# A fused eight-layer kernel: two PSUM banks for the scan's turned states, its end states kept by ScalarE, the causal mask added by VectorE, and another order for the feed-forward parts beside the scan

## The reference, cut to what matters

```python
x = x + _L0_attn_a_ref(_layernorm(x), ...)   # attention, 32 heads of 16
x = x + _L0_ffn_ref(_layernorm(x), ...)      # feed-forward, 1376 inner columns
x = x + _L0_attn_b_ref(_layernorm(x), ...)   # state-space layer with a scan
x = x + _L0_ffn_ref(_layernorm(x), ...)      # the same feed-forward again
x = x + _L1_attn_a_ref(_layernorm(x), ...)   # grouped attention, 32 heads of 128, rotary, causal
x = x + _L1_ffn_ref(...)                     # routed low-rank layer
x = x + _L1_attn_b_ref(...)                  # gated layer that zeroes the smaller half
x = x + _L1_ffn_ref(...)

# the scan of _L0_attn_b_ref: 1024 channels x 16 states, 512 tokens in order
def step(state, inp):
    dt_t, B_t, C_t, u_t = inp
    dA = jnp.exp(dt_t[..., None] * A)
    state = state * dA + (dt_t * u_t)[..., None] * B_t[:, None, :]
    y = jnp.einsum('bdn,bn->bd', state, C_t)
    return (state, y)

# the feed-forward, and the mask of _L1_attn_a_ref
gate = silu(x @ w_gate.T + b_gate); up = x @ w_up.T + b_up
out = (gate * up) @ w_down.T + b_down
scores = scores + jnp.where(qpos[:, None] >= kpos[None, :], 0.0, finfo(float32).min)
```

## Time and profile before

| | |
|---|---|
| median of 3 runs | 3086.19 us (3082.8 to 3101.64) |
| the profiled execution | 3082.76 us, its span 3081.0 us |
| granted TensorE clock over the span | 0.885 of full speed |
| busy over the span | PE 2444.4, DVE 2010.7, ACT 1585.7, POOL 1151.9 us |

### The profile page before, as it was taken

One profiled execution on the slowest core, in us unless ns is written; L12 is line 12 of the kernel. 1 busy time (PEld: TensorE's weight loads), 2 busy tenths in 40 slices (PEclk: granted clock), 3 DMA queues, 4 the chain that ended last, 5 costly groups with the idle time before them and its releaser, 6 DMA issues.

```text
span 3081.0 us, 36657 instructions
## 1 busy us (share of the span) xinstructions
PE 2444.4 (79%) x12408; PEld 1919.7 (62%) x12408; DVE 2010.7 (65%) x3083; ACT 1585.7 (51%) x3190; POOL 1151.9 (37%) x1016
## 2 busy tenths in 40 slices
PE   6986989677678857867889799999799999952058
PEld 4334358566667646756678678887678877842046
DVE  4724743587677569767754567775667774498894
ACT  1641640366665236666621166664366664599701
POOL 3011046051122424112247547565555754510071
PEclk8887899788898979888999999999899999976579
DMA  6123223110100111010023202111111112200011
GB/s 216 43 90 90 43 69 93 42 45 4 61 22 25 48 53 34 11 59 21 22 61 93 76 25 59 45 52 52 48 35 49 59 45 59 69 28 0 0 31 45
DMA packets 87696, 155.72 MB, mean 51 GB/s; under 512 B 8824, under 2 KB 17656, under 8 KB 87384
## 3 DMA queue, kind: packets, MB, share of 16 engines
q1 hardware_dynamic: 87512, 153.38, 17.2%
HBM read 138.21 MB, written 14.75 MB: 50 GB/s over the span
## 4 chain that ended last, share of the span: by engine, by line
PE 36%; ACT 9%; DVE 5%; issue 4%; POOL 2%; POOLq 0%; ACTq 0%; DVEq 0%
PE ps L623 33%; ACT tables L1290 5%; PE ps L637 3%; ACT m L1173 1%; POOL w_lo L567 1%; ACT tables L1145 1%; POOL w_hi L566 1%; POOL k L580 1%; DVE stat L1344 0%; DVE tables L1767 0%; DVE hT_lo L1357 0%; DVE f_lo L1329 0%; DVE x_sb L1332 0%; DVE f_hi L1328 0%; ACT m L1155 0%
## 5 line engine op out<-in xcount | busy, mean ns | idle before, releaser
L566 POOL TENSOR_SCALAR w_hi<-w_in 128x512 fp32r<-128x512 f32 x430 | 324.6, 755 | 1387.8 <-PE ps L623 822.3
L567 POOL TENSOR_TENSOR w_lo<-w_in,w_hi 128x512 fp32r<-128x512 f32 x430 | 614.1, 1428 | 35.9
L623 PE MATMUL ps<-hT_hi,w_lo 128*128 128x512 f32 x864 | 352.9, 408 | 22.9 <-DVE a L1374 12.5
L1533 DVE TENSOR_TENSOR_SCAN m<-m,m 128x1028 f32<-128x1028 f32 x128 | 307.8, 2404 | 69.7 <-ACT m L1173 62.3
L637 PE MATMUL ps<-tables,m 128*128 128x128 f32 x1024 | 186.1, 311 | 205.4 <-ACT tables L1145 121.0
L623 PE MATMUL ps<-hT_hi,w_hi 128*128 128x512 f32 x864 | 341.9, 396 | 0.0
L623 PE MATMUL ps<-hT_lo,w_hi 128*128 128x512 f32 x864 | 341.4, 395 | 0.0
L623 PE MATMUL ps<-m,tables 128*128 128x128 f32 (+1 forms) x2112 | 323.5, 302 | 12.7 <-ACT tables L1145 12.0
L623 PEld LDWEIGHTS ps<-m,tables 128*128 128x128 f32 (+1 forms) x2112 | 293.5, 213 | 22.6 <-ACT tables L1145 16.3
L637 PEld LDWEIGHTS ps<-tables,m 128*128 128x128 f32 x1024 | 128.5, 157 | 241.3 <-ACT tables L1145 144.5
L1145 ACT ACTIVATE tables<-ps 128x512 f32<-128x512 f32 x256 | 150.7, 589 | 189.0 <-PE ps L637 185.5
(11 more groups left out here) (245 smaller groups left out, 5470.4 us busy)
## 6 DMA issues: line engine op xcount, KB each, us to landing
w_in<-units SPq DMA_DIRECT2D x430, 256.0 KB, 2.6
stack_scratch<-a SPq DMA_DIRECT2D x48, 256.0 KB
a<-stack_scratch SPq DMA_DIRECT2D x64, 192.0 KB, 4.5
m<-bc_scratch SPq DMA_DIRECT2D x16, 512.0 KB, 5.3
out<-x_sb SPq DMA_DIRECT2D x2, 1024.0 KB, 4.3
tables<-small SPq DMA_DIRECT2D x1, 1399.0 KB, 10.5
x_sb<-x SPq DMA_DIRECT2D x4, 256.0 KB, 3.6
x_sb<-x SPq DMA_DIRECT2D x1, 1024.0 KB, 7.6
```

Source lines behind the costliest of these rows:

```text
L566: c["did"](nc.gpsimd.tensor_scalar(w_hi[:, r], raw, 1.0, 1.0, ALU.mult, ALU.mult), s["unit_hi"])
L567: c["did"](nc.gpsimd.tensor_tensor(w_lo[:, r], raw, w_hi[:, r].bitcast(F32), ALU.subtract), s["unit_split"])
L623: ins = T.matmul(out, lhsT, rhs, start=start, stop=stop)
L1533: V.tensor_tensor_scan(states, m_dA[:, dA:dA + NG].rearrange("p a t -> p (a t)"), states, 0.0, ALU.mult, ALU.add)\
```

## The change

Scan:

- the turned states of part 0 stay in bank 6, those of part 1 go to bank 5; the up projection beside the scan moves from bank 5 to bank 4, where it follows the gate;
- `m_dA` has 3 groups of buffers, and ACT makes the decays of group n+1 in group n's turn, ahead of both copies of turned states of n-2;
- the end states of the first half are kept by ACT (`last_kept`) and put back by ACT (in `decays`); both DVE copies are gone;
- the time steps of the second half's first tiles are made during the last tile of the first half, as between any tiles;
- on DVE `skip` comes behind the next group's inputs.

Feed-forward: the gate is an item of its own (`fgate`), and the order on PE is gate k, down k-1, up k everywhere. ACT's silu stands at the up item. Beside the scan `at_ends` puts the parts [gate k, down k-1], [up k], [multiply k] in the middle and at the end of the 16 tiles; of the second batch's scan, block 0 now stands ahead of the scan.

Grouped attention: the mask matmuls are gone, and DVE adds the mask to the last 128 columns of t = 1, 2, 3 in PSUM (`hide`) before the maxima.

To make room, `m_ssmT` and `m_v` lie over the routing weights, and one table (`Bw`) is loaded again ahead of the grouped attention, whose first users wait for it.

```diff
+            s += [[("fgate", b, k, up)], [("fproj", b, k, up)], [("fmul", b, k, up)]] if k < FK else []
+            s[-3 if k < FK else -1] += [("fdown", b, k - 1)] if k else []
...
+    def at_ends(scans, parts):
+        out, done, ends = [], 0, 2 * DT
+        for n, item in enumerate(scans):
+            out.append(item)
+            tile, last = divmod(n, N_ST // QS)
+            want = (2 * tile + last + 1) * len(parts) // (2 * ends) if last else done + ((tile + 1) * len(parts) // ends - tile * len(parts) // ends) // 2
+            out += flat(parts[done:want])
+            done = want
+        return out + flat(parts[done:])
...
-    s += front(1) + ln(0) + mix(scan(1), ffn(0))
+    s += front(1) + ln(0) + flat(ffn(0)[:3]) + at_ends(scan(1), ffn(0, 4)[3:])
...
-                if q == 0 and i % 2 and i + 1 < DT:
+                if q == 0 and i % 2 and (half, i) != (1, DT - 1):
                     time_steps(i + 1)
...
-                    o, slot = claim(6, s["m_hT_kept"]), n % G_RING * NG + 2 * part
+                    o, slot = claim(6 - part, s["m_hT_kept"]), n % G_RING * NG + 2 * part
...
+                def last_kept(n):
+                        act.wait_ge(s["m_h"], n + 1)
+                        go(A(m_last[:, st:st + NG].unsqueeze(2), m_st[:, slot:slot + NG, HL:SEG], ACT.Copy), s["m_last_kept"])
...
+                def decays(n):
+                    if n >= DA_RING:
+                        act.wait_ge(s["m_h"], n - DA_RING + 1)
+                    if at >= DT * N_ST // NG:
+                        act.wait_ge(s["m_last_kept"], lasts_kept(n - DT * N_ST // NG))
+                        go(A(m_st[:, slot:slot + NG, 0:1], m_last[:, st:st + NG].unsqueeze(2), ACT.Copy), s["m_dA"])
+                    for r in range(NG):
+                        go(A(m_dA[:, n % DA_RING * NG + r, 1:SEG], m_dt[:, tile % 4], ACT.Exp, scale=negA[:, st:st + 1]), s["m_dA"])
...
                 for g in range(q * QS // NG, (q + 1) * QS // NG):
                     n = scan_group(b, half, i, g)
-                    if n - 2 >= first:
-                        states_kept(n - 2, 0)
+                    decays(n + 1)
+                    last_kept(n - 2)
                     if i == 0:
                         diagonal(g)
                     if n - 2 >= first:
+                        states_kept(n - 2, 0)
                         states_kept(n - 2, 1)
...
-                    if held:
-                        skip()
                     after = following(g)
                     if after[1:] != (0, 0):
                         inputs(*after)
-                    if half == 0:
-                        did(V.tensor_copy(m_last[:, at:at + NG].unsqueeze(2), m_st[:, slot:slot + NG, HL:SEG]))
+                    if held:
+                        skip()
...
-                            mm(o[:, t * P:w], ident_r[:, :], mask_r[:, :], False, True, s["g_scores"])
...
                 def maxima_2():
                     need(s["g_scores"])
+                    go(hide(2))
+                    need(s["g_scores"])
+                    did(hide(3))
                     go(top(2))
-                    need(s["g_scores"])
                     did(top(3))
```

More of the change, by code:

```diff
@@ L59 @@
 SEG = HL + 1
-G_RING = 3
+G_RING, DA_RING = 3, 3
 G_KEEP = G_REP + 2
@@ L82, in schedule, with ffn, flat @@
     s = []
-    def ffn(b):
+    def ffn(b, up=5):
         s = []
         for k in range(FK + 1):
-            s += [("fproj", b, k), ("fmul", b, k)] if k < FK else []
-            s += [("fdown", b, k - 1)] if k else []
-        return s
+            s += [[("fgate", b, k, up)], [("fproj", b, k, up)], [("fmul", b, k, up)]] if k < FK else []
+            s[-3 if k < FK else -1] += [("fdown", b, k - 1)] if k else []
+        return s
+    def flat(parts):
+        return [item for part in parts for item in part]
     def scan(b):
@@ L156, in item_units @@
         return [("ao", c) for c in range(HC)]
+    if kind == "fgate":
+        return [("fg", item[2])]
     if kind == "fproj":
-        return [("fg", item[2]), ("fu", item[2])]
+        return [("fu", item[2])]
     if kind == "fdown":
@@ L194, in scan_group, with decays_made, lasts_kept @@
     return ((2 * b + half) * DT + i) * (N_ST // NG) + g
+def decays_made(n):
+    per = DT * N_ST // NG
+    return NG * (n + 1) + n // (2 * per) * per + max(n % (2 * per) + 1 - per, 0)
+def lasts_kept(n):
+    per = DT * N_ST // NG
+    return n // (2 * per) * per + min(n % (2 * per) + 1, per)
 def columns(widths):
@@ L328, in hybrid_layers @@
         m_acc = cut("m_front", 1024, 2)
-        m_ssmT = cut("m", 512)
+        m_ssmT, m_v = (small[:, SMALL["route_A"][0] + 512 * n:SMALL["route_A"][0] + 512 * (n + 1)] for n in range(2))
+        m_v = m_v.rearrange("p (a c) -> p a c", a=2)
         m_ssm, m_sq = cut("m_front", TT * 64, TT), cut("m_front", TT * 64, TT)
@@ L1144, in states_kept @@
                         act.wait_ge(s["m_y"], 2 * n + part - 1)
-                    go(A(m_hT[:, part], ps[:, 6], ACT.Copy), s["m_hT_kept"])
+                    go(A(m_hT[:, part], ps[:, 6 - part], ACT.Copy), s["m_hT_kept"])
                 def diagonal(g):
@@ L1597, in top, with hide @@
                     return V.reduce_max(g_max[:, t:t + 1], ps[:, bank, at_s:at_s + (t + 1) * P] if src is None else src, AX.X)
+                def hide(t):
+                    bank, at_s = g_bank[t]
+                    own_keys = ps[:, bank, at_s + t * P:at_s + (t + 1) * P]
+                    return V.tensor_tensor(own_keys, own_keys, col("mask"), ALU.add)
                 def shifts(t):
```

106 lines of the change are left out of this document (55 added, 51 removed).

## The result

The changed kernel takes 3064.61 us (median of 8 runs, 3053.74 to 3075.57), the kernel before beside it 3086.69 us (8 runs, 3076.89 to 3115.04). The ratio is 0.9918, with a 95% interval of 0.9893 to 0.9944. The forecast was 2980, a fall of 106 us; a fifth of it came, and the time lies above the range. The profiled execution took 3064.25 us, its span 3062.5, against 3081.0 before.

What follows compares the result with a forecast made beforehand. Scans were bound by no engine (DVE nearest), other stages by PE. 3081 - 107 (scans) + 3 (second scan's start) + 9.5 (feed-forward) - 11.5 (mask) = 2975 span, 2980 as median; range 2925 to 3045.

Steps and rivals of the forecast that it cites:

- What bounds the kernel: Whole kernel: in the scans no engine is full, DVE nearest; feed-forward alone and grouped attention are set by PE.
- Scan, DVE's work: Each scan: both copies leave DVE, saving 15 us (8 to 22.8), so its work falls from 307.5 to 292.5 us.
- Scan, DVE's idle time: Each scan: DVE's idle time falls from 96.5 to 58 us, the sum of 8, 12, 16 and 22.
- Skip: Scans: DVE's skip, moved behind the next inputs, waits 8 us for PE's outputs instead of 31 (bounds 0 and 16).
- Decays: Scans: decays made a group ahead cut the scan's wait for ACT from 31 to 12 us (5 to 20).
- Silu, time steps, start of the second half: Scans: DVE's remaining waits at these places fall from 34 to 16 us (10 to 26).
- New wait at the inputs: Scans: DVE's inputs wait for turned states behind PE's double feed-forward blocks, 22 us (0 to 70).
- Scan, ACT and banks: Scans: ACT's 64 added small copies, at most 19 us, fit its idle time; 3.2 us per group against DVE's 3.5.
- ACT's order: Scans, rival: copies behind four decays close a ring, 5.2 us per group, 428 per scan, 3135 in all; chance 0.04.
- Start of the second scan: Ahead of the second scan: gate 0, up 0 and the multiply lengthen the chain by 3 us (0 to 8).
- Feed-forward alone: Outside the scans: PE stalls 0.5 us for f_lo's split in each of 9 + 10 blocks, +9.5 us (0 to 19).
- Mask: Grouped attention: 192 matmuls less on PE, -11.5 us; DVE's 192 additions, 54 us, fit its idle time.

Runs made afterwards that it cites:

- e9: Kernel before, with the feed-forward taken out of the scans and put behind each: 3091.55 us (one run); first scan 315.3 us.
- e10: Changed kernel, but DVE again keeps and puts back the end states, as before: 3058.01 us, ratio 0.9886.
- e6: Changed kernel, but ACT makes both copies of turned states and its copy of the end states ahead of decays and diagonals: 3022.32 us, ratio 0.9778.
- e12: Changed kernel with e1, e2, e6 and e7 together, and one feed-forward part behind each scan item: 2971.58 us, ratio 0.9612.
- e7: Changed kernel, but the time steps' product is made at the end of the tile before, ahead of the feed-forward part: 3044.9 us, ratio 0.9851.
- e4: Changed kernel, but down k-1 stands with the multiply everywhere, so PE's blocks beside the scans are single ones of 12 matmuls: 3081.5 us, ratio 0.9972.
- e1: Changed kernel, but SP asks for three more weight units ahead of the transfers that broadcast B and C: 3065.75 us, ratio 0.9919.
- e11: Changed kernel, but second batch's block 0 is inside the scan again, and the first scan's last multiply stands earlier: 3083.97 us (one run).
- e2: Changed kernel, but the feed-forward that stands alone has its old order on PE (gate k, up k, down k-1): 3049.7 us, ratio 0.9868.
- e5: Changed kernel, but both parts of the turned states go to bank 6, as before the change: 3153.79 us, ratio 1.0203.

## Why the prediction was wrong

**What bounds the kernel.** Right: the scans are nobody's, heads and feed-forward are PE's. Missed: how poor the scans' overlap is. The earlier trace rows had the sign of it: 404 us with 302 of PE, and ten blocks beside it of some 8 us of PE each; I never asked what the scan would take without them. e9 says 315, so the last 82 us of that scan are bought at full price.

**Scan, DVE's work.** Forecast 292.5, measured 294.5. Right. But that the time would fall with it was assumed; in e10 DVE has 6.6 us more of it and the scans are no longer (2 us less, within what they vary), with ACT's order as in the change.

**Scan, DVE's idle time: the step that failed.** Forecast 58, measured 83.5. The forecast took it that decays ahead of both copies cost nothing, since ACT's 3.2 us of a group fit into DVE's 3.5; with the copies first (e6) a scan is 17.5 us shorter, out of 28 that each scan misses. By its terms, in the second scan (they add up to 81.8 of its 87.8 us of idle time):

- *Skip*, forecast 8, measured 23.9. I took 1.2 us off each of 13 waits and let PE "come sooner once it need not wait for its bank". It did not: PE now waits for ACT's copies at the outputs. But late copies are not the whole cause. With the copies first the skip still waits 27.6 (e6) and 29.3 (e12), so the 8 was wrong for a reason that no run here isolates.
- *Decays*, forecast 12, measured 2.1. Right and better than forecast. It was got by putting them first on ACT, which the inputs paid for; e6 has them second at 7.3.
- *Silu, time steps, start of the second half*, forecast 16, measured 10.8 + 14.6 = 25.4. The boundary itself did go as said: 11.0 us from scan to scan instead of 23.7.

```profile
1339.95 2.30 DVE L1582 TENSOR_TENSOR_SCAN m<-m,m 128x1028 f32<-128x1028 f32 x1
...
1350.97 3.26 DVE L1582 TENSOR_TENSOR_SCAN m<-m,m 128x1028 f32<-128x1028 f32 x1
```

  What was not seen is that the product for each next pair of tiles stands behind a block of 24 feed-forward matmuls at some places (e7: 9 us a scan). That is no fault of the change alone: ACT waited 28.1 us for it before and 40.6 after. The forecast let this wait shrink, and it grew.
- *New wait at the inputs*, forecast 22, measured 21.7 + 8.7 = 30.4. The first part is what was forecast in size, but not by its cause: with blocks of half the length it is 23.8 (e4), and e6, which leaves the blocks alone, takes it down to 6.5. The 8.7 is the wait for ACT's copy of the end states, which stands behind the decays; in e6 it is 1.3. I had priced that copy by its length and not by its place in the queue.

**Scan, ACT and banks.** The size was right (19 at most). The small copies take 0.2 us, 12.7 us in a scan:

```profile
L1213 ACT ACTIVATE m<-m 128x4 f32<-128x4 f32 x32 | 6.5, 205 | 10.7 <-DVE m L1536 5.9 <-DVE m L1582 4.5
L1175 ACT ACTIVATE m<-m 128x4 f32<-128x4 f32 x32 | 6.2, 195 | 0.0
```

The rule was wrong. The rival *ACT's order* I gave 0.04, since ACT's share of a group (3.2 us) stays below DVE's 3.5. That is a mean over an undisturbed group. At a time step or a silu ACT has some 10 us in one piece (1187.52 to 1197.62 above), and there the copies wait behind all of it; e6 shows 17.5 us a scan for the order. So it was a milder form of the rival, not the closed ring of 5.2 us in each group. That the 17.5 us lie at the places with a time step or a silu (7 and 10 in a scan) is my reading of the one place shown; no run separates them.

**Start of the second scan.** Forecast +3, measured +15.2. PE comes to gate 0 with nothing split:

```profile
1131.70 0.62 POOL L594 TENSOR_SCALAR w_hi<-w_in 128x512 fp32r<-128x512 f32 x1 [58.88 <-DMA w_in<-units]
```

```profile
1122.99 11.03 SPq L482 DMA_DIRECT2D w_in<-units  x5
```

```profile
1133.76 0.76 PE L651 MATMUL ps<-hT_hi,w_lo 128*128 128x512 f32 x1 [6.97 <-issue]
```

SP asks for these weights at 1122.99, behind the broadcasts of B and C, and they land 8.7 us later; the gate starts 7 us late, its first eight matmuls 0.43 us apart (0.23 later). e1 gives 5 of the 12 us back; the rest is the work itself, which e11 pays inside the scan (12.5) when it is not here. I counted the block as work of PE alone and not its weights' way through SP and POOL.

**Behind the scans, not priced:** +8.5 and +5.4. The last multiply and down stand behind the last scan item and must go through skip, DVE and PE one after the other. Here is that place in the first batch; in e12, where they stand ahead of the last scan item, these stretches are 69.8 and 81.7:

```profile
1005.64 0.69 DVE L1382 TENSOR_TENSOR f_lo<-loose,f_hi 128x512 fp32r<-128x512 f32 x1
```

```profile
1006.39 0.50 PE L651 MATMUL ps<-w_hi,f_lo 128*128 128x512 f32 x1 [2.55 <-DVE f_lo L1382]
```

**Feed-forward alone.** The mechanism was right, its size was not: 9.5 forecast, 10.4 measured in the two rows of blocks (+4.3, +6.1), and 6.4 more in what follows each. e2 gives all four back, so both are of the order; why the 6.4 arise was not looked into. PE's wait for f_lo is there as a row of its own, and PE is busy 82.8 of 87 us where it was 85.9 of 86:

```profile
PE ps L651 <- DVE f_lo L1382: 3.7, 7, 1.0
```

That is 0.5 us a time, as forecast, seven times in the stretch. f_lo's median over the kernel rose from 0.693 us to 0.978, with the same least and greatest values (0.691 and 1.666), and PE's wait for the line that makes it, over the kernel, from 2.6 to 18.5 us. The Trainium skill ("SBUF — State Buffer", Who interferes with whom) has DVE and GpSimd share a pair of ports under an exclusive lock. The two lengths of f_lo agree with that; no run here changes POOL's work to test it.

**Mask.** Right: -15.1 for -11.5. DVE's work in 25 heads rose from 195 to 222 us, the 192 additions of both batches took 0.289 to 0.300 us each, and PE is busy 275.5 of 280 where it was 276.0.

**The range.** The scans' miss of 57 alone gives 2980 + 57 = 3037, still inside. What took the time out is the 12 of the second scan's start, the 14 behind the scans and the 7 of the feed-forward, less 4 of the mask. The first two of these are also no loss of their own: e11 moves that work back inside, and the scans grow by nearly as much. What they share with the scans, as I read it, is that the place of an item in an engine's fixed order was taken as free. The prediction's own sign of being wrong, scans over 375 us, came true as well: the stretches that were 404 us in the earlier trace rows are 378.

## What to carry to other kernels

When an edit moves instructions on an engine that works in order, price what stands behind them at its busiest place (the one with table loads, a silu and a late product), not by the engine's mean share. A wait that goes at one instruction is only gone when the next user of the same data does not show it. And before forecasting what better overlap will give, run each part without the other: here next to nothing of the work beside the scan had been hidden (0 of 82 us, 6 of 85).

## What the runs showed of the hardware

- Three changes of table in one piece cost ACT 1.28 us each and no more: the logarithm ends at 1191.55, the load starts at 1191.57, the silu at 1192.86. The Trainium skill ("ScalarE: Activation LUTs", What ACT_TABLE_LOAD costs) gives 2.66 us for a change, with a drain of 1.38; here the drain does not show as time.
- With the feed-forward beside them, the scans had their highest granted clock where they were shortest: 0.87 in the change (378 us), 0.90 and 0.89 in e6 (360 and 361), 0.93 in e12 (354), so those spent more of their time at the 2.4 GHz level. It did not simply follow PE's idle time: with some 100 us of it the kernel before had 0.87 and 0.88, e4 0.84 and 0.85, and e5, with 122 and 124 us of it, 0.86. How much of e12's gain is the clock, no run separates.
- After 6.97 us without work the first matmuls of gate 0 start 0.43 us apart, at a granted clock of 0.50 (1133.7 to 1136.8), the 1.2 GHz level; from 1137.20 on they start 0.23 apart, at 1.00, the 2.4 GHz level.
